# One DMA transpose for the high and low halves, and a new order of rows, scales and copies in an attention layer of one core

## The reference

```python
x = x + LN(attn(LN(x)))        # q, k, v = relu(h @ W + b); causal softmax(q k^T / sqrt(512)) v; relu(y @ Wo + bo)
x = x + LN(ffn(LN(x)))
# ffn: two gates. Each: 4 channels summed with weights to 1 (128 groups), batch norm over all 8192 rows,
# gelu, a linear map to 512, softmax, top 32 of 512. One gate masks the output of h @ W, the other the input of it.
```

## Time and profile before

| | us |
|---|---|
| runs of before | 2181.84, 2189.44, 2190.82; median 2189.44 |
| the profiled execution | 2195.03 |
| its span, first to last instruction | 2193.2 |

### The profile page before, as it was taken

How to read it: one execution, slowest core, us unless ns; L and a number is a source line. 1 busy time by engine, 2 the same in 40 slices (tenths; PEclk the granted TensorE clock), 3 DMA queues, 4 the chain that set the end, 5 groups by cost and what they waited for, 6 DMA issues and landing times. The chain is left out here.

```text
span 2193.2 us, 35462 instructions
## 1 busy us (share of the span) xinstructions
PE 2004.8 (91%) x11039; PEld 1108.7 (51%) x11039; DVE 1675.2 (76%) x3468; ACT 1146.6 (52%) x2496; POOL 1259.2 (57%) x1421
## 2 busy tenths in 40 slices
PE   7779999988999997899998888999899999999997
PEld 3445555554555555556555555644444444444443
DVE  8477665666866556776655767567999999999999
ACT  5344343343434334353333444333688888888885
POOL 6263443345434235452525446232699999999997
PEclk9899999999999999999999999999999999999999
DMA  6768566557775757667665666435132232323221
GB/s 210 188 146 184 145 152 133 147 161 171 154 158 126 158 131 191 156 153 179 128 155 138 175 168 149 135 96 163 44 96 92 87 102 83 106 83 97 92 87 63
DMA packets 387920, 295.05 MB, mean 135 GB/s; under 512 B 276370, under 2 KB 304658, under 8 KB 387732
## 3 DMA queue, kind: packets, MB, share of 16 engines
q1 hardware_dynamic: 362388, 212.03, 37.8%
q10 hardware_dynamic: 25344, 80.75, 14.3%
HBM read 165.27 MB, written 64.23 MB: 105 GB/s over the span
## 5 line engine op out<-in xcount | busy, mean ns | idle before, releaser
L725 PE MATMUL psum<-v,pT 128*128 128x512 f16 x1632 | 367.6, 383 | 13.8 <-DMA pT<-rows 13.8
L725 PE MATMUL psum<-kT,qT 128*128 128x512 f16 (+3 forms) x1920 | 369.0, 351 | 1.8 <-DVE kT L1435 1.8
L745 PE MATMUL psum<-hT_early,ring 128*128 128x256 f16 x2160 | 254.6, 278 | 40.9 <-ACT part L1062 36.5
L1416 DVE SCALAR_TENSOR_TENSOR part<-psum,part 128x512 f32<-128x512 f32 x180 | 123.9, 688 | 208.9 <-ACT part L1062 114.2
L725 PEld LDWEIGHTS psum<-kT,qT 128*128 128x128 f16 x1920 | 182.9, 99 | 182.5 <-issue 9.2
L725 PEld LDWEIGHTS psum<-v,pT 128*128 128x128 f16 x1632 | 160.1, 98 | 199.9 <-issue 22.9
L745 PEld LDWEIGHTS psum<-hT_early,ring 128*128 128x128 f16 x2160 | 212.6, 99 | 82.9 <-ACT part L1062 41.8
L745 PE MATMUL psum<-hT_late,ring 128*128 128x256 f16 x1620 | 205.0, 290 | 51.9 <-issue 37.5
L1807 DVE MAX8 c<-cut 128x8 f32<-128x512 f32 x384 | 245.5, 683 | 0.0
L1062 ACT ACTIVATE part<-psum,bqkv_s 128x256 f32<-128x256 f32 x360 | 147.5, 467 | 151.9 <-PE psum L745 151.7
L745 PEld LDWEIGHTS psum<-hT_late,ring 128*128 128x128 f16 x1620 | 166.1, 104 | 93.0 <-issue 57.6
(11 more groups left out here) (198 smaller groups left out, 3821.2 us busy)
## 6 DMA issues: line engine op xcount, KB each, us to landing
ring<-wc_scratch ACTq DMA_DIRECT2D x132, 512.0 KB, 4.2
xg<-x SPq DMA_DIRECT2D x64, 256.0 KB, 4.7
xr<-x SPq DMA_DIRECT2D x64, 256.0 KB, 3.8
h_scratch<-hb SPq DMA_DIRECT2D x64, 256.0 KB, 3.4
h<-h_scratch SPq DMA_DIRECT2D x64, 256.0 KB, 2.8
x<-x_scratch SPq DMA_DIRECT2D x64, 256.0 KB, 3.0
x_scratch<-xr SPq DMA_DIRECT2D x62, 256.0 KB, 2.6
out<-zn SPq DMA_DIRECT2D x59, 256.0 KB, 2.0
```

Source lines behind the costliest of these rows:

```text
L725: mm = nc.tensor.matmul(outp, stat(a), mov(c), start=(n == 0 and k == 0), stop=(n == total - 1 and k == 2))
L745: mm = nc.tensor.matmul(P_BANKS[p][:, 256 * m:256 * (m + 1)], ring[:, p, a, c, P * m:P * (m + 1)], h[:, b, c, :], start=(first and m + c + ...
L1416: nc.vector.scalar_tensor_tensor(part[:, n, :], P_BANKS[p], sign * QKV_DOWN, part[:, n, :], ALU.mult, ALU.add) \
```

## The change

Five edits:

1. **One transpose for both halves.** `phl` and `pT` hold high and low of a chunk side by side, so one DMA transpose of up to 128 x 1024 replaces two of up to 128 x 512; the same for `hhl` and `hT_early`, `hT_late`. 160 + 105 transposes stand where 320 + 210 stood. Bytes are the same.
2. **SP's order.** In h = 7 the transposes of q = 4, 5, 6 go ahead of those of T0's rows. `load_x` for the next group goes from h = 0 to the end of h = 1, behind the transposes of T1's rows.
3. **ScalarE's copies first.** In h = 2 and 4 `copy_5` and the refill of the weight ring go ahead of the exponential.
4. **GpSimd's scales first.** `difference` 7 goes from the end of h = 5 to h = 6, behind the scales; the three `lo_h` of q = 4, 5, 6 go from the end of h = 6 to h = 7, behind `attention_scale` and `second_scale` and ahead of `residual`.
5. **Fourth tile's convolution.** For T3, `convolution` goes from lag 3 (h = 1) to lag 5 (h = 3), with `channel_sum`, `store_h2` and `store_xc` one and two half-stages behind it. For the last T3 but one these come after the loop.

```diff
+def due_conv(H, behind):
+    for lag, fourth in ((3, False), (5, True)):
+        T = due(H, lag + behind)
+        if T is not None and (T % GROUP == GROUP - 1) == fourth:
+            return T
+    return None
...
-            pT = sa("pT", [P, 4, 2, 512], F16)
+            pT = sa("pT", [P, 4, 1024], F16)
...
-                        for a in range(2):
-                            dst = hT_early[:, g % 2, q, a] if q < 4 else hT_late[:, q - 4, a]
-                            sp.dma_start_transpose(dst.rearrange("p c (t n) -> p (c t) n", t=2), hhl[:, q % 4, a, :]) \
-                                .then_inc(hT_in[(0, 0, 1, 1, 2, 2, 3)[q]].sem, 16)
+                        dst = hT_early[:, g % 2, q] if q < 4 else hT_late[:, q - 4]
+                        sp.dma_start_transpose(dst.rearrange("p a c (t n) -> p (a c t) n", t=2),
+                                               hhl[:, q % 4].rearrange("p a n -> p (a n)")) \
+                            .then_inc(hT_in[(0, 0, 1, 1, 2, 2, 3)[q]].sem, 16)
...
-                        for a in range(2):
-                            sp.dma_start_transpose(pT[:, n % 4, a, 0:w].rearrange("p (c n) -> p c n", n=P), phl[:, n % 4, a, 0:w]) \
-                                .then_inc(pT_in[n % 4].sem, 16)
+                        sp.dma_start_transpose(pT[:, n % 4, 0:2 * w].rearrange("p (c n) -> p c n", n=P), phl[:, n % 4, 0:2 * w]) \
+                            .then_inc(pT_in[n % 4].sem, 16)
...
-                    for lag, move in ((-1, load_residual), (2, store_x1), (4, store_h2), (5, store_xc)):
-                        if due(H, lag) is not None:
-                            move(due(H, lag))
+                    for T, move in ((due(H, -1), load_residual), (due(H, 2), store_x1), (due_conv(H, 1), store_h2),
+                                    (due_conv(H, 2), store_xc)):
+                        if T is not None:
+                            move(T)
...
-                    if h == 0 and 0 < g and g + 1 < NG:
+                    if h == 1 and 0 < g and g + 1 < NG:
                         for j in range(GROUP):
                             load_x(g + 1, j)
...
+                    if h == 7 and g + 1 < NG:
+                        transpose_h(g + 1, 4, 5, 6)
                     if h == 7 and g < NG:
                         transpose_p(GROUP * g)
-                    if h == 7 and g + 1 < NG:
-                        transpose_h(g + 1, 4, 5, 6)
...
                         if kind:
                             copy_1(kind, g)
-                        exponential(s)
-                        if kind:
                             copy_5(kind, g)
                             refill(kind, g, 0)
+                        exponential(s)
                         hi_p(s, first)
...
-                        late(H, (3, convolution), (1, attention_stats), (2, residual_stats))
+                        if due_conv(H, 0) is not None:
+                            convolution(due_conv(H, 0))
+                        late(H, (1, attention_stats), (2, residual_stats))
...
                         second_scale(due(H, 2))
+                    if h == 6 and g + 1 < NG:
+                        difference(g + 1, 7, (1, 0), (0, 0), (1, 0))
+                    if h == 7 and g + 1 < NG:
+                        for q in (4, 5, 6):
+                            lo_h(g + 1, q)
                     if due(H, 1) is not None:
                         residual(due(H, 1))
-                    if due(H, 4) is not None and due(H, 4) < OWN:
-                        channel_sum(due(H, 4))
+                    if due_conv(H, 1) is not None and due_conv(H, 1) < OWN:
+                        channel_sum(due_conv(H, 1))
...
                     if h == 5 and g + 1 < NG:
                         lo_h(g + 1, 3)
-                        difference(g + 1, 7, (1, 0), (0, 0), (1, 0))
-                    if h == 6 and g + 1 < NG:
-                        for q in (4, 5, 6):
-                            lo_h(g + 1, q)
+                channel_sum(TS - 5)
```

More of the change, by code:

```diff
@@ L310, in layer_block @@
         sS = rows[:, 0:2 * S].rearrange("p (b n) -> p b n", b=2)
-        phl = rows[:, 2 * S:2 * S + 2048].bitcast(F16).rearrange("p (j a n) -> p j a n", j=4, a=2)
+        phl = rows[:, 2 * S:2 * S + 2048].bitcast(F16).rearrange("p (j n) -> p j n", j=4)
         w_first = rows[:].bitcast(F16).rearrange("p (a w c n) -> p a w c n", a=2, w=3, c=C)
-        hT_first = pT[:].rearrange("p j a n -> p (j a n)").rearrange("p (a c n) -> p a c n", a=2, c=C)
+        hT_first = pT[:].rearrange("p j n -> p (j n)").rearrange("p (a c n) -> p a c n", a=2, c=C)
         raw = part[:, 0:2, :]
@@ L331, in layer_block @@
         xg_in = [sig(f"xg_in{j}", 16) for j in range(GROUP)]
-        hT_in = [sig(f"hT_in{j}", step) for j, step in enumerate((64, 64, 64, 32))]
+        hT_in = [sig(f"hT_in{j}", step) for j, step in enumerate((32, 32, 32, 16))]
         wc_out, mix_ok = sem("wc_out"), sem("mix_ok")
-        pT_in = [sig(f"pT_in{j}", 32) for j in range(4)]
+        pT_in = [sig(f"pT_in{j}", 16) for j in range(4)]
         xr_in = [sig(f"xr_in{j}", 16) for j in range(4)]
@@ L682, in _ @@
                 store_x1(TS - 4)
+                store_h2(TS - 5)
+                store_xc(TS - 5)
                 load_residual(TS - 1)
@@ L832, in product @@
                     for k in range(width(T, j) // P):
-                        mm = three(Y_BANK[T % 2], GROUP * j + k, t + 1, lambda a: pT[:, n % 4, a, P * k:P * (k + 1)],
+                        mm = three(Y_BANK[T % 2], GROUP * j + k, t + 1, lambda a: pT[:, n % 4, width(T, j) * a + P * k:width(T, j) * a + P * (k + 1)],
                                    lambda a: v[:, a, GROUP * j + k, :])
@@ L1121, in hi_p @@
                         need(act, pT_in[n % 4], n // 4 - 1)
-                        nc.scalar.activation(phl[:, n % 4, 0, 0:w], sS[:, T % 2, 512 * j:512 * j + w], ACT.Copy, scale=P_SCALE) \
+                        nc.scalar.activation(phl[:, n % 4, 0:w], sS[:, T % 2, 512 * j:512 * j + w], ACT.Copy, scale=P_SCALE) \
                             .then_inc(p_hi.sem, 1)
@@ L1497, in lo_p @@
                         dve.wait_ge(p_hi.sem, p_hi.at(n))
-                        nc.vector.scalar_tensor_tensor(phl[:, n % 4, 1, 0:w], sS[:, T % 2, 512 * j:512 * j + w], P_SCALE,
-                                                       phl[:, n % 4, 0, 0:w], ALU.mult, ALU.subtract).then_inc(p_lo.sem, 1)
+                        nc.vector.scalar_tensor_tensor(phl[:, n % 4, w:2 * w], sS[:, T % 2, 512 * j:512 * j + w], P_SCALE,
+                                                       phl[:, n % 4, 0:w], ALU.mult, ALU.subtract).then_inc(p_lo.sem, 1)
                 def bias_o(T):
@@ L1642, in _ @@
                         score_rows(s)
-                        late(H, (3, convolution))
+                        if due_conv(H, 0) is not None:
+                            convolution(due_conv(H, 0))
                     elif h == 1:
```

## The result

The changed kernel takes **2181.61 us** (median) beside 2189.68 us for the kernel before on the same chips: a ratio of 0.9954, 95% interval 0.9940 to 0.9967 (taken over all runs; that of the two medians is 0.9963). That is 8 to 10 us faster, where 64 were forecast; the time lies above the range's upper end of 2176 us. The profiled execution has a span of 2179.9 us (before: 2193.2).

A forecast was written before the change was run, and what follows sets the result against it. TensorE, busy 1307 of 1426 us, bounds the loop of groups. Idle time 65.2 plus clock 20.9 less costs 22.4 gives 63.7 us, from a median of 2189.4 to 2126 us; range 2102 to 2176 us.

The forecast's parts named there:

- The rows behind P: `load_x` behind P's four transposes: VectorE waits for x, TensorE loses about 1 us in groups 4, 8, 12, 3 us.
- slower rival: VectorE held by loads of x behind merged transposes, needing landings of about 13 us; 2205 us, chance 0.06.
- SyncE's order and merging at v's products 4 to 6: Transposes of q = 4 to 6 issued ahead of T0's rows, and merged: 30.3 of 37.5 us of TensorE's waits gone.
- 3.2 us of landing: Time from issue to landing taken for the transpose of q = 5, in groups 8 and 13, ahead of v's products.
- A merged transpose: SyncE's issue of one transpose of 1024 columns: taken as 1.3 us, with 2.6 us (proportional) as the other end.
- The rival by which it costs two: A merged transpose takes 2.6 us of issue, what two did; 48 us gained, 2141 us, chance 0.05.
- Scales first: GpSimd's `attention_scale` starts when VectorE is done, so stalls at v's product 3 shorten or vanish: 23.3 us gained.
- T3's and T1's rows: Half the issues precede the last chunk, so transposes of these rows land sooner: 8 of 13.8 us gained, ends 4 and 13.8.
- `copy_5` first: Product 4 of q no longer waits, product 5 still needs `copy_u2`: 3.6 us in three groups, ends 0 and 12.3.
- The clock: Low clock costs 57 us in the loop; 0.32 us regained per us of stall removed, 20.9 us, ends 10 and 31.
- The convolution: 3.4 us of VectorE in h = 3 delays k's first products (10.4 us) and the freeing of product 2's bank (9 us).
- The end: Seam to the second phase: half the issues gain nothing; T3's moved steps feed only memory and sums, no cost counted.

The follow-up runs named there:

- e5: The changed kernel with the loads of x for the next group back in h = 0, ahead of P's transposes: 2142.59 us, ratio 0.9781.
- e10: The kernel before with one edit alone, the rows of x loaded in h = 1 behind P's transposes: 2237.71 us, ratio 1.0218.
- e3: The changed kernel with v's second ring refill moved to the start of h = 1, behind the late transposes: 2167.35 us, ratio 0.9896.
- e12: e6 with GpSimd's order of before (`difference` 7 in h = 5, low halves in h = 6 behind `residual`): 2147.62 us, ratio 0.9806.
- e1: The kernel before with merged transposes for both halves and nothing else of the change: 2178.18 us, ratio 0.9942.
- e13: e9 with `copy_5` and the ring's first refill back behind the exponential in h = 2 and 4: 2138.02 us, ratio 0.9763.
- e9: e6 with GpSimd's channel sum of TS - 5 put behind the scales and residual in the tail: 2114.39 us, ratio 0.9658.
- e6: The changed kernel with rows of x loaded in h = 0 and v's second refill at the start of h = 1: 2116.65 us, ratio 0.9662.
- e8: e6 with the fourth tile's convolution back in h = 1, with its stores and channel sum: 2122.46 us, ratio 0.9690.
- e4: The changed kernel with GpSimd's channel sum of TS - 5 put behind the scales and residual in the tail alone: 2177.02 us, ratio 0.9937.
- e2: The changed kernel with the fourth tile's convolution, its stores and channel sum back in h = 1: 2168.47 us, ratio 0.9917.
- e7: The changed kernel with a transpose for each half, as in the kernel before, all else kept: 2250.56 us, ratio 1.0270.

## Why the prediction was wrong

The sign was right and the size was not. By its own steps:

**The rows behind P: priced at 3 us, they cost 39 (e5); alone, 46 (e10). This is the step that failed.** Three errors lie in it. It took "four transposes, 5.2 us" for P in group 8, four issues of 1.3; they took 7.85, since one waited 1.2 us for VectorE's low half of its chunk and the last took 2.68 us to issue, so the rows left 2.6 us later against P than computed. It put a cost on groups 4, 8 and 12 alone; VectorE waited in 23 places, and in the short groups, where no bank runs short, the wait goes on through the row maxima, the exponential and `copy_u2` to q's product 5. And it counted VectorE's time without the convolution as room, though everything behind the means stood still. The prediction named the mechanism as its slower rival and asked for landings of 13 us; the landings of these loads were 2.8 to 5.9 us. The cause was the issue, not the landing.

**SyncE's order and merging at v's products 4 to 6: 30.3 us forecast, -0.7 found.** The issue came as computed: in group 13, 1.1 us of scales and 2.6 of low halves were to lie between VectorE's moments and the transpose of q = 5, and 3.68 us did (1174.63 to 1178.31). The term that failed is "3.2 us of landing". It is the median of all 210 transposes of h, and it mixes two kinds: the 68 with no load of the ring in flight landed after 2.4 us, the 142 others after 4.8. The new order asks for a refill within 1 us of the first late one in groups 2 to 13. The trace of before shows what that can cost, had I looked at what else was in flight. Its group 13, SyncE, ScalarE's queue and TensorE:

```profile
1192.75 7.79 SPq L542 DMA_TRANSPOSE hT_late<-hhl  x6
...
1198.00 0.33 ACTq L1100 DMA_DIRECT2D ring<-wc_scratch  x1
...
1204.55 6.10 PE L745 MATMUL psum<-hT_late,ring 128*128 128x256 f16 x36 [5.28 <-issue]
```

Of the six, the one issued at 1196.62 landed at 1204.46, after 7.8 us, and the refill at 1204.43. The Trainium skill, page "DMA: Bandwidth & Descriptors", section "Issuing engines are not separate DMA queues", says that DMAs run on the same 16 engines and interleave, whichever engine started them; e3 agrees (8.8 and 3.1 us for the same transpose). In the large groups, 3, 4, 7, 8 and 12, the wait fell to 0 as forecast.

**A merged transpose: 1.3 us forecast, 1.26 measured** (median of 112 of 1024 columns; 1.24, 1.22 and 1.20 for 768, 512 and 256). A half of 512 columns took 1.27 before. The rival by which it costs two is out. The Trainium skill, page "DMA: Bandwidth & Descriptors", section "Why a DMA increments its semaphore by 16 and not by 1", gives one push for each tile for "previous generations"; the trace does not agree with what the prediction made of it, since 256 columns more cost 0.02 us. What no row told: beside a refill an issue can block; the longest of h took 6.37 us.

**Scales first: 23.3 us forecast, 24.7 found** (34.4 to 9.7 at products 0 to 3; 22.2 at product 3 alone, 30.3 to 8.2), and 24.0 in e12. In group 10 GpSimd's scale starts 0.19 us behind VectorE's moments. This chain was read step by step from the earlier trace rows, and it held.

**T3's and T1's rows: 8 us forecast for merging.** The waits did fall by 10, but merging alone raised T3's by 12 (e1); ScalarE's order took them away (e13). Right size, wrong cause. **`copy_5` first: 3.6 us forecast, 24 found** (e13, with the refill, on e9), for the same reason: I priced it at the product that waits for the copy, and what it frees is the path from exponential to P.

**The clock: 20.9 us forecast in all, 0.32 for each us of stall.** From before to the change TensorE's busy time in the loop fell by 14.7 us, beside only 6.3 us less idle time; from before to e6 by 29.9 beside 52.5, 0.57 for each. So the size came out near, without the stalls that it was to follow from, and no fixed ratio shows. The 57 us also rest on a rounded 0.96: the clock of 0.964 in the loop makes it 51.

**The convolution: 19.4 us forecast as a cost.** The waits at k did grow by 17 us, from 6.2 to 23.1: 10.8 of the 23.1 wait for VectorE's sums, where the 19.4 were to come, and the waits for ScalarE's copies at product 3, which the sum did not have, grew from 6.2 to 12.3. What it freed in h = 1, 13 us at q with early rows (e8), was not in the sum: the move is worth 6 us. **The end: forecast nothing, 7.1 us found**: 2.5 of idle time, 1.9 of them by the channel sum (e4, e9), and 4.6 of busy time at a lower clock, whose cause stays open. Three kernels with the sum where it was before took 35.4 to 37.1 us against 34.6 (e1, e2, e8), with 1.1 us of idle time in each: that is clock alone. "Feeds only memory and the sums" is true of its output, not of its place in GpSimd's list.

So the large terms that were read as chains held, that of v's products once the refill was out of the way, and e6 (2116.65 us) shows what the change is worth without its two collisions. Either repair alone would have put the time inside the stated range (e5 2142.59, e3 2167.35 us).

## What to carry to other kernels

When a load is moved behind a step, time it by when that step's last piece is *ready*, not by the issue cost of its instructions; then follow the waiting engine's list to everything behind it, in every kind of group. Before taking a median landing for a transfer that is moved, look at what will be in flight beside it at its new place, on the other queues too. And try two repairs together before judging either: here 39 and 14 us apart made 65.

## What the runs showed of the hardware

In group 13 a transpose issued 0.7 us ahead of a 0.5 MB load of another queue landed after 8.8 us, where the same one without that load took 3.1 (e3), and the load took 7.9 us against a median of 4.1. With the load 0.0 to 0.4 us behind, most first transposes landed after 5.3 to 5.8 us. The third transpose in a row held SyncE's queue for 5.3 to 6.4 us in groups 2, 5, 9 and 13 of the kernel after; the pairs of e7 showed no late one above 2.5 us and none at all above 2.9, those of the kernel before up to 4.8. By the medians an issue of a transpose costs SyncE 1.2 to 1.3 us, whether it moves 256 or 1024 columns.
